# A load of 1 MB moved behind the stores of the query tiles in two cross-attention passes

## The chip, the cores and the metric

The kernel runs on one core of one Trainium2 chip. The metric is the device time of one execution in microseconds, taken as the median of several runs. The core has five engines that work side by side and meet through semaphores: PE (TensorE, the matmuls), DVE (VectorE), ACT (ScalarE), POOL (GpSimd) and SP (SyncE). SP computes nothing: it waits for semaphores and issues DMAs, strictly in the order of its program.

## What is computed

Two sequences of 2048 tokens with 512 channels go through two layers. `x` is (2, 2048, 512) and the context is (2, 77, 512). Cut to what matters, with the conditioning vectors left out:

```
# layer 0: cross-attention
q = ada_ln(x) @ Wq + bq                       # 16 heads of 32
x = x + softmax(q k^T / sqrt(32)) v @ Wp + bp # k, v from the 77 context tokens
# layer 1
q, k, v = split(modulate(ln(x)) @ qkv_w + qkv_b)
x = x + gate * (mha(q, k, v) @ self_o_w + self_o_b)   # 2048 x 2048 self-attention
q = ln(x, g, b) @ q_w + q_b
x = x + mha(q, k_ctx, v_ctx) @ cross_o_w + cross_o_b  # cross-attention again
x = x + gate * (gelu(modulate(ln(x)) @ w1 + b1) @ w2 + b2)
```

## The kernel before

The program is a chain of stages: `conditioning`, `cross_pass` "p1" (layer 0; called pass 1 here), `dense_pass` (q, k and v of the self-attention), `attention`, `cross_pass` "p3" (called pass 3: output projection of the self-attention, then the cross-attention of layer 1) and `mlp`. The change touches `cross_pass` alone, in both of its forms: `own is None` is pass 1, the other form is pass 3.

`cross_pass` works on N = 8 chunks of 512 tokens. A chunk goes through several steps: load of its rows x, (pass 3: projection of the self-attention's output, `own_row`, added to x by `add_own`), statistics and normalisation, turn to channels-first, projection of the queries in four tiles, scores, softmax, weighing of the values, projection of the output, added to x by `add_out`, second normalisation for the next stage. The steps of several chunks are interleaved by hand. Slot m runs the scores of chunk m, the output of chunk m - 1, the projection of the queries of chunk m + 1 and the loads of chunk m + 2. Every engine has its own `slot(m)`, a list of steps in a fixed order, and an engine never goes past a step that waits. The slots of the engines are offset against one another: what DVE does at the start of its slot m + 1 falls into the same time as what SP and PE do at the end of theirs.

x has XR = 3 buffers of 1 MB. Chunks 0 to 2 are loaded ahead of the slots, and `load_x(m + 2)` in the slots m = 1 to 5 loads the chunks 3 to 7: five loads in each pass. `load_x(n)` (L401 to L406) waits until the buffer's former rows are stored and normalised a second time (`xn_done[1]`, a POOL step). Its users are: in pass 1 DVE's `statistics(1, n, 0..3)` (L1138), which stand in DVE's slot n - 1 right behind `query_rest(n-1, 2)`, with `out_rest(n-2, 1)` (L1114) between the first and the second of them; in pass 3 POOL's `add_own_row(n)` (L1418), then DVE's `add_own(n, 0..3)` (L1129).

The queries of a chunk go out and come back through HBM. PE projects a tile (L564), ACT writes its high part into `qo[:, t % 2]` (`query`, L853), DVE the low part (`query_rest`, L1118), and `store_q(n, t)` (L417, 0.5 MB) stores it as soon as `taken["query"]` says so. ACT's `query(n, t)` with t >= 2 waits until the store of tile t - 2 has landed, since they share a buffer. `load_q(n, g)` (L428, three DMAs of 0.25 MB) waits for the landing of the store and loads the tile head by head into `qs[:, g % 2]`, from which PE's `scores` (L590) read. `store_u` (L439 and L440, two DMAs of 0.25 MB) stores the second normalisation's result, after POOL's `rest(2, ...)` (L1428).

On PE, near the end of the slot: `query(m+1,3)`, `turn_weights` of the heads 10 and 11, `turn(2,m-1,1)`, `turn_weights(m,12)` (L601, needs ACT's copy `et` of head 10), `weigh(m,2)` (L610, needs `et` and DVE's `out_rest(m,1)` through the semaphore `os_lo`), `turn_weights(m,13)`, then `scores(m+1,0)`. In pass 3, PE's slot holds `own_row(m+1, 1..3)` (L542 on `p_oi`) between the scores; there are two banks for all projections, and `own_row(n, 2)` needs the bank that DVE's `add_own(n, 0)` frees.

Of the kernel before, what the change touches and what calls it, by code (L numbers as in the profile page):

```python
# [33 lines left out]
def channels(ap):  # L34

    return ap.rearrange("(t p) n -> p t n", p=P)
# [272 lines left out]
def cross_pass(nc, d, name, x_in, x_out, own, k_in, v_in, q_mid, norm_q, norm_u, q_bias, b_out, u_out, raw, preload):  # L309
# [7 lines left out]
    XR = 3  # L317
# [3 lines left out]
    has = lambda n: 0 <= n < N  # L321
# [15 lines left out]
    with nc.cleanup_on_exit(), ExitStack() as ctx:  # L337
# [60 lines left out]
        @block.sync  # L398
        def _(sp):
            def load_x(n):  # L400
                b, i = place(n)  # L401
                if n >= XR:

                    sp.wait_ge(x_stored[n % XR], DMA * (n // XR))
                    sp.wait_ge(xn_done[1], (n - XR + 1) * TT)
                sp.dma_start(x[:, n % XR], x_in[b, i * W:(i + 1) * W, :].rearrange("(t p) c -> p t c", p=P)).then_inc(x_in_s[n % XR], DMA)  # L406

            def load_own(n):
                b, i = place(n)
                if n > 0:  # L410
                    sp.wait_ge(projected["own"], n * TT)
                sp.dma_start(oi.raw[:], o_in[b, :, i * W:(i + 1) * W].rearrange("(t p) w -> p t w", p=P)).then_inc(own_in, DMA)

            def store_q(n, t):
                b, i = place(n)
                sp.wait_ge(taken["query"], n * KT + t + 1)
                sp.dma_start(q_mid[:, b, t * P:(t + 1) * P, i * W:(i + 1) * W].rearrange("s p w -> p s w"),  # L417
                             qo[:, t % 2].bitcast(F32)).then_inc(q_stored[t % 2], DMA)

            def load_q(n, g):  # L420
                b, i = place(n)
                sp.wait_ge(q_stored[g % 2], DMA * ((n * G + g) // 2 + 1))
                if n * G + g >= 2:

                    sp.wait_ge(sm_done, (n * G + g - 1) * TT)
                for row, part in enumerate((0, 0, 1)):
                    src = q_mid[part, b, g * P:(g + 1) * P, i * W:(i + 1) * W].rearrange("(h r) w -> r h w", h=GH)
                    sp.dma_start(qs[row * DH:(row + 1) * DH, g % 2].bitcast(F32), src).then_inc(q_loaded[g % 2], DMA)  # L428

            def store_x(n):  # L430
                b, i = place(n)
                sp.wait_ge(taken["out"], (n + 1) * TT)
                sp.dma_start(x_out[b, i * W:(i + 1) * W, :].rearrange("(t p) c -> p t c", p=P), x[:, n % XR]).then_inc(x_stored[n % XR], DMA)

            def store_u(n, t):
                b, i = place(n)
                r = (n * KT + t) % UR
                sp.wait_ge(u_lo[1], n * KT + t + 1)
                sp.dma_start(u_out[0, b, t * P:(t + 1) * P, i * W:(i + 1) * W], ut.hi[:, r].bitcast(F32)).then_inc(u_stored[r], DMA)  # L439
                sp.dma_start(u_out[1, b, t * P:(t + 1) * P, i * W:(i + 1) * W], ut.lo[:, r].bitcast(F32)).then_inc(u_stored[r], DMA)  # L440

            def slot(m):
                if own is None:
                    if has(m - 3):
                        store_u(m - 3, 3)
                    if has(m):
                        load_q(m, 1)
                        load_q(m, 2)
                    if has(m - 2):
                        store_u(m - 2, 0)  # L450
                    if has(m):
                        store_q(m, 3)
                        load_q(m, 3)
                    if has(m - 2):
                        store_u(m - 2, 1)
                    if has(m - 1):
                        store_x(m - 1)
                    if has(m + 1):
                        store_q(m + 1, 0)
                    if has(m + 2) and m + 2 >= XR:  # L460
                        load_x(m + 2)
                    if has(m - 2):
                        store_u(m - 2, 2)
                    if has(m + 1):
                        store_q(m + 1, 1)
                        load_q(m + 1, 0)
                        store_q(m + 1, 2)
                else:
                    if has(m - 2):
                        store_u(m - 2, 1)  # L470
                    if has(m + 2) and m + 2 >= 1:
                        load_own(m + 2)
                    if m + 2 == CHUNKS:

                        sp.wait_ge(projected["own"], CHUNKS * TT)
                        sp.dma_start(raw.raw[:, 0], channels(own_weight)).then_inc(w_again, DMA)
                    if has(m - 1):
                        store_x(m - 1)
                    if has(m + 1):
                        store_q(m + 1, 0)  # L480
                    if has(m - 2):
                        store_u(m - 2, 2)
                    if has(m + 2) and m + 2 >= XR:
                        load_x(m + 2)
                    if has(m + 1):
                        store_q(m + 1, 1)
                        load_q(m + 1, 0)
                        load_q(m + 1, 1)
                    if has(m - 2):
                        store_u(m - 2, 3)  # L490
                    if has(m + 1):
                        store_q(m + 1, 2)
                    if has(m - 1):
                        store_u(m - 1, 0)
                    if has(m + 1):
                        load_q(m + 1, 2)
                        store_q(m + 1, 3)
                        load_q(m + 1, 3)
                if m == 0:
                    for dst, src in preload:  # L500
                        sp.dma_start(dst, src).then_inc(preloaded, DMA)

            with nc.allow_non_contiguous_dma(reason="short vectors, once"):
                if own is not None:
                    for b in range(B):
                        sp.dma_start(grow[:, b], gate[b].partition_broadcast(P)).then_inc(grow_in, DMA)
                    load_own(0)
                load_x(0)
                for dst, src in small:
                    sp.dma_start(dst, src).then_inc(small_in, DMA)  # L510
                load_x(1)
                for row, part in enumerate((0, 1, 0)):
                    for b in range(B):
                        sp.dma_start(ks[row * DH:(row + 1) * DH, b, :, 0:S].bitcast(F32),
                                     k_in[part, b].rearrange("(h r) s -> r h s", r=DH)).then_inc(ks_in, DMA)
                sp.dma_start(v[0:S], v_in.rearrange("b s c -> s b c")).then_inc(ks_in, DMA)
            load_x(2)
            for m in SLOTS:
                slot(m)
            for r in range(XR):  # L520
                sp.wait_ge(x_stored[r], DMA * len(range(r, N, XR)))
            for r in range(UR):
                sp.wait_ge(u_stored[r], 2 * DMA * len(range(r, N * KT, UR)))
            sp.wait_ge(preloaded, DMA * len(preload))
# [1956 lines left out]
```

## Time and profile before

| | us |
|---|---|
| median of 3 runs | 3903.49 |
| lowest and highest | 3900.64, 3904.45 |
| the profiled execution | 3910.66 |
| its span, from first to last instruction | 3908.9 |
| PE busy in it | 3628.2 (93%) |
| mean granted clock of PE | 0.95 |
| pass 1, about | 87 to 596 |
| pass 3, about | 2600 to 3190 |

A profile tells of one execution; its times are counted from the start of the span. Rows of a timeline give start, duration, engine, line, operation, written tile, read tiles and a count, and in brackets how long the engine had been idle and what ended that. SPq is the queue of SyncE, and its rows are the moments of issue; a merged row (x3) runs from the first issue to the end of the last. In names, `p_` stands for both passes: `p_x` is a chunk's rows, `p_qo` the projected tile, `s_q` its place in HBM, `p_qs` the loaded queries, `p_sm` scores, `p_tr` and `p_et` turned weights, `p_acc` weighed values, `p_os` their two parts, `p_pp` a projection.

### The profile page before, as it was taken

What the parts mean: (1) busy time and instruction counts of PE and PEld (TensorE: products, weight loads), DVE (VectorE), ACT (ScalarE), POOL (GpSimd) and SP (SyncE); (2) the same over time, 40 slices, a digit from 0 to 9 for tenths busy, and PEclk for the clock granted to TensorE, in tenths of its full rate; (3) what the DMA queues carried; (4) which work ended last, traced back from release to release, by engine and by line L of the source; (5) the groups of instructions that cost most, each with busy time, mean ns of one, the idle gap of its engine ahead of it and who ended that gap; (6) DMA issues with size and microseconds to landing.
All of it is one profiled execution on the core that took longest, in us unless ns stands there. A gap on an engine that the chain in (4) does not pass through costs nothing. (4 is left out here: it accounts for less than half of the span.)

```text
span 3908.9 us, 50109 instructions
## 1 busy us (share of the span) xinstructions
PE 3628.2 (93%) x18828; PEld 2403.3 (61%) x18828; DVE 2226.6 (57%) x3964; ACT 1870.3 (48%) x3442; POOL 2132.5 (55%) x1063
## 2 busy tenths in 40 slices
PE   5699988999999999999999999968999969999999
PEld 2577766875555555555555554426777748888887
DVE  2466652266777777777777777614766633222222
ACT  1455552115666666666666666644556532111111
POOL 0456540005898888889888888865677520000000
PEclk8798888999999999999999999987999879999999
DMA  7655657755555555555555554444575661111110
GB/s 231 154 157 149 177 146 221 241 176 141 125 120 120 127 127 132 128 124 118 120 127 130 128 131 103 116 132 110 149 181 157 159 206 58 49 44 44 44 44 33
DMA packets 232009, 505.92 MB, mean 129 GB/s; under 512 B 38199, under 2 KB 55095, under 8 KB 211799
## 3 DMA queue, kind: packets, MB, share of 16 engines
q1 hardware_dynamic: 213335, 368.49, 34.6%
q0 software_dynamic: 18432, 134.23, 15.7%
q8 instruction: 149, 2.44, 0.3%
q14 instruction: 93, 0.76, 0.1%
HBM read 215.54 MB, written 144.51 MB: 92 GB/s over the span
## 5 line engine op out<-in xcount | busy, mean ns | idle before, releaser
L2117 DVE TENSOR_REDUCE first_peak<-first_sm 128x1 f32<-128x512 f32 x1963 | 1211.1, 680 | 358.7 <-PE first_sm L1947 357.5
L2077 ACT ACTIVATE a_e<-a_st 128x512 f32<-128x512 f32 x2048 | 1061.7, 603 | 534.7 <-PE a_st L1966 523.5
L2177 POOL TENSOR_TENSOR a_esum<-a_esum,a_e 128x2048 f32<-128x2048 f32 x256 | 1208.8, 4722 | 18.5
L1966 PE MATMUL a_st<-first_q,first_k 128*128 128x512 f32 x2048 | 825.5, 406 | 16.8 <-ACT a_e L2077 12.0
L1947 PE MATMUL first_sm<-first_k,first_q 96*128 96x512 f32 x1963 | 833.1, 424 | 0.0
L1947 PEld LDWEIGHTS first_sm<-first_k,first_q 96*128 96x128 f32 x1963 | 369.9, 188 | 425.2 <-DVE first_peak L2117 316.2
L1979 PE MATMUL a_acc<-a_e,a_v 128*32 128x512 f32 x4096 | 505.7, 600 | 0.0
L1966 PEld LDWEIGHTS a_st<-first_q,first_k 128*128 128x128 f32 x2048 | 387.6, 190 | 131.2 <-ACT a_e L2077 51.7
L2365 ACT ACTIVATE mlp_gelu<-mlp_ph,mlp_b 128x512 f32<-128x512 f32 x128 | 88.3, 690 | 590.0 <-PE mlp_ph L2327 590.0
L2419 POOL TENSOR_TENSOR mlp_x<-mlp_x,mlp_brow 128x2048 f32<-128x2048 f32 x8 | 39.5, 4934 | 581.7 <-DMA mlp_x<-s_x 581.7
L2327 PE MATMUL mlp_ph<-mlp_us,mlp_w_hi 128*128 128x512 f32 x1024 | 336.6, 391 | 19.2 <-DMA mlp_us<-s_u 19.2
L2380 DVE CAST mlp_gs<-mlp_gelu 128x512 fp32r<-128x512 f32 x128 | 54.8, 428 | 462.2 <-ACT mlp_gelu L2365 462.2
L2339 PE MATMUL mlp_py<-mlp_w_hi,mlp_gs 128*128 128x512 f32 x1024 | 315.3, 389 | 1.8 <-DVE mlp_gs L2382 1.8
L1434 POOL TENSOR_TENSOR p_e<-p_e,p_inv 128x308 f32<-128x308 f32 x256 | 173.4, 711 | 172.0 <-DVE p_inv L1110 172.0
L1979 PEld LDWEIGHTS a_acc<-a_e,a_v 128*32 128x32 f32 x4096 | 100.4, 108 | 220.2 <-ACT a_e L2077 125.1
L2327 PEld LDWEIGHTS mlp_ph<-mlp_us,mlp_w_hi 128*128 128x128 f32 x1024 | 193.5, 189 | 60.0 <-issue 19.6
L590 PE MATMUL p_sm<-p_ks,p_qs 96*128 96x78 f32 x1024 | 170.5, 309 | 53.0 <-DMA p_qs<-s_q 32.2
L2339 PEld LDWEIGHTS mlp_py<-mlp_w_hi,mlp_gs 128*128 128x128 f32 x1024 | 192.1, 188 | 42.0 <-issue 2.1
L590 PEld LDWEIGHTS p_sm<-p_ks,p_qs 96*128 96x128 f32 x1024 | 155.8, 220 | 85.9 <-DMA p_qs<-s_q 31.1
L2327 PE MATMUL mlp_ph<-mlp_us,mlp_raw_lo 128*128 128x512 f32 x512 | 200.2, 391 | 0.0
L2339 PE MATMUL mlp_py<-mlp_raw_lo,mlp_gs 128*128 128x512 f32 x512 | 199.2, 389 | 0.0
L1095 DVE TENSOR_REDUCE p_top<-p_sm 128x4 f32<-128x308 f32 x256 | 118.1, 464 | 138.2 <-PE p_sm L590 136.3
(161 smaller groups left out, 5317.2 us busy)
## 6 DMA issues: line engine op xcount, KB each, us to landing
a_esum_moved<-a_e POOLq DMA_DIRECT2D x128, 1024.0 KB, 7.3
p_qs<-s_q SPq DMA_DIRECT2D x192, 256.0 KB, 5.9
s_q<-p_qo SPq DMA_DIRECT2D x64, 512.0 KB, 7.6
first_k<-s_k SPq DMA_DIRECT2D x24, 1024.0 KB, 11.0
first_q<-s_q SPq DMA_DIRECT2D x96, 256.0 KB, 7.1
s_x<-p_x SPq DMA_DIRECT2D x16, 1024.0 KB, 4.4
s_u<-p_ut_hi SPq DMA_DIRECT2D x64, 256.0 KB, 5.8
s_u<-p_ut_lo SPq DMA_DIRECT2D x64, 256.0 KB, 6.4
```

Source lines behind the costliest of these rows:

```text
L590: mm = pe.matmul(sm[:, unit % 2, h * KE:(h + 1) * KE], qs[0:3 * DH, g % 2, h, qt * P:(qt + 1) * P], ks[0:3 * DH, b, g * GH + h], start=Tru ...
L1095: dve.tensor_reduce(top[:, unit % 4], src, AX.X, ALU.max).then_inc(top_done, 1)
L1434: pool.tensor_tensor(e[:, number % 2, qt, :, 0:S], e[:, number % 2, qt, :, 0:S], inv[:, number % 2, qt].unsqueeze(2).to_broadcast([P, GH, ...
L1947: mm = pe.matmul(sm[:, bank_of_unit(j, u), x * KE:(x + 1) * KE], q[0:3 * DH, j % QR, h, qt * P:(qt + 1) * P], k[0:3 * DH, g % 2, h, kc * K ...
L1966: pe.matmul(st[0:KR, place(kt, h) % RING], k[:, g % 2, h, kt * P:kt * P + KR], q[:, j % QR, h], start=True, stop=True).then_inc(score_done, 1)
L1979: mm = pe.matmul(acc[rows, 0], v[0:KR, g % 2, kt, rows], e[0:KR, (j * NKT + kt) % ER, h], start=(kt == 0), stop=(kt == NKT - 1), tile_posi ...
L2077: act.activation(e[0:KR, (j * NKT + kt) % ER, h], st[0:KR, place(kt, h) % RING], ACT.Exp, scale=SCALE).then_inc(score_read, 1)
L2117: dve.tensor_reduce(dst, src, AX.X, ALU.max).then_inc(unit_read, 1)
L2177: pool.tensor_tensor(esum[:], e[:, slot(0)] if x == 1 else esum[:], e[:, slot(x)], ALU.add).then_inc(e_added, 1)
L2327: mm = pe.matmul(ph[:, m % 4], w1[pw][:, t, m * P:(m + 1) * P], us[:, n % 2, pm, t], start=(t == 0 and s == 0), stop=(t == KT - 1 and s == 2))
L2339: mm = pe.matmul(py[:, tt], gs[:, m % 2, pw, tt * P:(tt + 1) * P], w2[pm][:, m], start=(m == 0 and s == 0), stop=(m == HT - 1 and s == 2))
L2365: act.activation(gelu[:, m % 2], ph[:, m % 4], ACT.Gelu_apprx_tanh, bias=b1[:, m:m + 1]).then_inc(gelu_done, 1)
```

## The change

In both forms of SP's `slot(m)` the call `load_x(m + 2)` moves down. In pass 1 it stood behind `store_q(m+1,0)` and stands behind `store_q(m+1,2)`, as the last of the slot; `store_q(m+1,1)` and `load_q(m+1,0)` also move ahead of `store_u(m-2,2)`. In pass 3 it stood behind `store_u(m-2,2)` and stands behind `store_q(m+1,2)`, ahead of `store_u(m-1,0)`. No instruction is added or taken away, and no wait.

```diff
@@ SP's slot, own is None (pass 1)
                     if has(m + 1):
                         store_q(m + 1, 0)
+                        store_q(m + 1, 1)
+                        load_q(m + 1, 0)
+                    if has(m - 2):
+                        store_u(m - 2, 2)
+                    if has(m + 1):
+                        store_q(m + 1, 2)
                     if has(m + 2) and m + 2 >= XR:
                         load_x(m + 2)
-                    if has(m - 2):
-                        store_u(m - 2, 2)
-                    if has(m + 1):
-                        store_q(m + 1, 1)
-                        load_q(m + 1, 0)
-                        store_q(m + 1, 2)
@@ SP's slot, the other form (pass 3)
                         store_q(m + 1, 0)
                     if has(m - 2):
                         store_u(m - 2, 2)
-                    if has(m + 2) and m + 2 >= XR:
-                        load_x(m + 2)
                     if has(m + 1):
                         store_q(m + 1, 1)
                         load_q(m + 1, 0)
...
                         store_u(m - 2, 3)
                     if has(m + 1):
                         store_q(m + 1, 2)
+                    if has(m + 2) and m + 2 >= XR:
+                        load_x(m + 2)
                     if has(m - 1):
                         store_u(m - 1, 0)
```

## Rows read from the trace of the kernel before

**Rows 1.** The page: the span, and busy time of the engines.

```profile
span 3908.9 us, 50109 instructions
...
PE 3628.2 (93%) x18828; PEld 2403.3 (61%) x18828; DVE 2226.6 (57%) x3964; ACT 1870.3 (48%) x3442; POOL 2132.5 (55%) x1063
```

**Rows 2.** Table of windows: busy us of each engine, granted clock, DMA share.

```profile
core 0: us, PE busy (x) PEld busy (x) DVE busy (x) ACT busy (x) POOL busy (x), PEclk, DMA share, GB/s
212.00:270.00 58.00, 55.68 (x352) 44.44 (x350) 41.98 (x96) 38.36 (x77) 40.02 (x37) 0.97 0.60 164
386.00:444.00 58.00, 53.42 (x289) 42.49 (x288) 35.38 (x78) 33.09 (x65) 33.82 (x33) 0.82 0.63 164
...
2880.00:2940.00 60.00, 56.82 (x328) 45.53 (x326) 37.14 (x78) 34.38 (x65) 41.64 (x40) 0.94 0.69 168
402.50:422.30 19.80, 19.79 (x77) 14.79 (x78) 8.74 (x20) 12.77 (x24) 7.50 (x8) 0.50 0.69 179
2912.00:2920.90 8.90, 8.87 (x42) 8.00 (x43) 6.52 (x12) 3.14 (x7) 2.74 (x3) 0.62 1.05 219
```

**Rows 3.** Table of waits in pass 1: us in total, times, longest.

```profile
ACT p_qo L853 <- DMA s_q<-p_qo: 29.0, 6, 6.4
...
PE p_tr L601 <- ACT p_et L814: 18.4, 8, 4.7
```

**Rows 4.** The same table in pass 3.

```profile
PE p_sm L590 <- DMA p_qs<-s_q: 15.6, 7, 4.2
```

**Rows 5.** Timeline of SyncE's queue, slot 4 of pass 1: start, us.

```profile
389.57 0.37 SPq L406 DMA_DIRECT2D p_x<-in_x  x1
...
391.01 0.87 SPq L417 DMA_DIRECT2D s_q<-p_qo  x1
...
394.26 0.65 SPq L417 DMA_DIRECT2D s_q<-p_qo  x1
...
401.23 1.30 SPq L428 DMA_DIRECT2D p_qs<-s_q  x3
```

**Rows 6.** Timelines of ACT, DVE and PE in the same slot.

```profile
401.29 0.69 ACT L853 ACTIVATE p_qo<-p_pp,p_qb 128x512 fp32r<-128x512 f32 x1 [6.36 <-DMA s_q<-p_qo]
...
389.15 0.74 DVE L1118 SCALAR_TENSOR_TENSOR p_qo<-p_pp,p_qb,p_qo 128x512 fp32r<-128x512 f32 x1
...
395.93 0.69 DVE L1138 BATCH_NORM_STATS2 p_stats<-p_x 128x6 f32<-128x512 f32 x1 [2.08 <-DMA p_x<-in_x]
396.54 0.67 DVE L1114 TENSOR_TENSOR p_os<-p_acc,p_os 128x512 fp32r<-128x512 f32 x1
...
402.51 1.14 PE L601 MATMUL p_tr<-p_ident,p_e 128*77 128x128 f32 x4 [4.58 <-ACT p_et L814]
403.58 1.94 PE L610 MATMUL p_acc<-p_et,p_v 77*32 77x512 f32 x8
```

**Rows 7.** The store of L417 issued at 394.26: its time to landing.

```profile
DMA to landing us min/median/max: 12.2/12.2/12.2
```

**Rows 8.** Timelines of ACT and PE in slot 6, pass 1.

```profile
510.44 0.69 ACT L853 ACTIVATE p_qo<-p_pp,p_qb 128x512 fp32r<-128x512 f32 x1 [1.73 <-PE p_pp L564]
...
512.25 1.06 PE L610 MATMUL p_acc<-p_et,p_v 77*32 77x512 f32 x8
```

**Rows 9.** Timelines, slot 3, pass 3: SyncE, its landing, POOL, DVE, PE.

```profile
2910.99 0.37 SPq L417 DMA_DIRECT2D s_q<-p_qo  x1
...
DMA to landing us min/median/max: 9.9/9.9/9.9
...
2907.31 4.97 POOL L1418 TENSOR_TENSOR p_x<-p_x,p_brow 128x512 f32<-128x512 f32 x4
...
2917.98 0.68 DVE L1129 TENSOR_TENSOR p_x<-p_pp,p_x 128x512 f32<-128x512 f32 x1
...
2912.03 1.08 PE L590 MATMUL p_sm<-p_ks,p_qs 96*128 96x78 f32 x8 [2.37 <-DMA p_qs<-s_q]
...
2922.78 0.48 PE L542 MATMUL p_pp<-p_w,p_oi_hi 128*128 128x512 f32 x1
```

More of the change, by code:

```diff
@@ L482, in slot @@
                         store_u(m - 2, 2)
-                    if has(m + 2) and m + 2 >= XR:
-                        load_x(m + 2)
                     if has(m + 1):
@@ L492, in slot @@
                         store_q(m + 1, 2)
+                    if has(m + 2) and m + 2 >= XR:
+                        load_x(m + 2)
                     if has(m - 1):
```

## Prediction, made before the changed kernel was run

> **What bounds the kernel now.** I read the page first, for where the time lies. TensorE (PE) is busy 93% of a span of 3908.9 us [rows 1], so nearly everything that makes PE wait is paid for. The change touches only `cross_pass`, which runs twice: pass 1 from about 87 to 596 us and pass 3 from about 2600 to 3190 us. The table of windows comes next: in a middle slot PE is busy 53.4 of 58 us in pass 1 and 56.8 of 60 us in pass 3 [rows 2]. Both passes are PE-bound, with little slack for a new stall. The table also gives the granted clock: 0.97 in pass 1's first slot with a load, 0.82 in a later one, 0.94 in pass 3.
>
> The table of waits then says what holds PE: in pass 1 mainly `turn_weights`, behind ACT's copies of `et` (18.4 us in 8 waits), and behind that ACT's `query` step, which waits for a store of `qo` (29.0 us in 6) [rows 3]. In pass 3 PE waits for the load of `qs`, 15.6 us in 7 [rows 4]. So the queue of SyncE (SP) matters, and the timelines of one slot, m = 4 of pass 1, show how. The load of x is issued at 389.57, the store of query tile 1 at 391.01, that of tile 2 at 394.26 [rows 5]. DVE finished tile 1 at 389.15 + 0.74 = 389.89 and gets x at 395.93, 6.3 us after the issue. ACT gets the buffer of tile 1 back only at 401.29, 10.2 us after its store was issued. PE then restarts at 402.51 after 4.58 us idle [rows 6]. Slot m = 6 has no load of x: there ACT waits 1.73 us, for PE, at the same step, and `weigh(m,2)` follows at 512.25 with no gap [rows 8]. So the load ahead of the stores does cost PE time, as the change assumes. What remains is what the load costs when it is late.
>
> **Part by part.** Nothing is added or removed: 5 loads of 1 MB per pass (rows 3 to 7, slots m = 1 to 5) move down SP's list, their two waits with them. Their own waits cost nothing in the new place, since POOL's normalise is done by then.
>
> *Pass 1.* The load moves past `store_q(m+1,1)`, `load_q(m+1,0)` (three DMAs), `store_u(m-2,2)` (two) and `store_q(m+1,2)`: 7 DMAs, 0.5 + 0.75 + 0.5 + 0.5 MB. `store_q(m+1,1)` can go at 389.9, 1.1 us earlier, with no load before it, so its buffer comes back before ACT asks, and the wait of 4.58 us is gone. What is late next is x. The load can be issued only behind `store_q(m+1,2)`, at about 394.7 instead of 389.57 [rows 5]. The transfers in front of it are the ones that were behind it. The queue was busy from 389.57 until tile 2's store landed, 12.2 us after 394.26, at 406.5 [rows 5, 7]. The new order moves the same bytes from 389.9 on, so the last of them, now x, lands at about 406.5 instead of 395.9. DVE's next instruction in order is `statistics(1,m+2,0)`, which needs x, and queued right behind it is `out_rest(m,1)`. Before, that one ended at 396.54 + 0.67 = 397.2, 1.3 us after x landed [rows 6]. PE's `weigh(m,2)` waits for it through `os_lo`, and all the scores of the next slot stand behind `weigh` on PE. So `weigh` goes from 403.58 [rows 6] to 406.5 + 1.3 = 407.8: +4.2 us. The bounds: if x took from its new issue only what it took at the head of the queue, 6.3 us, it would land at 401.0 and `weigh` would come at 402.3, -1.3 us. If the loads of `qs` that now come sooner behind it slow it by another 1 us (my guess), +5.2. I take 4.2, since the queue is full in either order. PE has no slack after that, so 5 x 4.2 = +21 us.
>
> The clock in pass 1: after the stall PE ran 19.8 us at 0.50, its lower level of 1.2 GHz [rows 2]. The later slots pay for such a stretch already, and the new gap of about 9 us keeps it. The first slot ran at 0.97 and would go to about 0.82: 58 x 0.15 = +9 us. Pass 1: +30 us.
>
> *Pass 3.* The load moves past `store_q(m+1,1)`, `load_q(m+1,0)` and `load_q(m+1,1)` (six DMAs), `store_u(m-2,3)` (two) and `store_q(m+1,2)`. In slot m = 3 the stores and loads of q gain, and PE's gap of 2.37 us before `scores` at 2912.03 goes [rows 9]. Tile 2's store landed 9.9 us after 2910.99, at 2920.9. By the same exchange x lands there, less 1 us because the two stores of `store_u(m-1,0)` that shared the queue with it now come later (estimate): 2919.9, where POOL had it in time for 2907.31. POOL is the first user: `add_own_row` takes 4.97 us for its four tiles, so it ends at 2924.9. DVE's `add_own(m+2,0)`, at 2917.98 before, follows and takes 0.68, and PE's `own_row(m+2,2)` needs that to free its bank: 2925.6 against 2922.78 before, +2.9 us [rows 9]. Behind POOL's wait stand `rest(2,m-1,0)` and so SP's `store_u(m-1,0)`, behind that `load_q(m+1,2)`. That load would land some 3 us before its scores, and I cost it at nothing; if that cover goes, each us late is one more on PE. The bounds: if the loads and stores of q go 5 us sooner than now, so that x follows at about 2906 instead of behind 2910.99, and x then takes only the 6.3 us of pass 1 [rows 6], it lands before 2913, `add_own` isn't held and PE keeps its gain. At the other end x lands 1 us later, +3.9. I take +2.9 x 5 = +14.5 us. Against pass 1, this point already contains the gain of the removed gap.
>
> The clock in pass 3: PE finishes what it can (`own_row(m+2,1)`, scores) and then stands some 8 us where it stood 2.4. A restart cost 8.9 x 0.38 = 3.4 us after the short gap in this slot and 19.8 x 0.5 = 9.9 us in pass 1 [rows 2]. I take 4, nearer to pass 3's own row, since dense matmuls follow at once: 5 x 4 = +20 us. Between the ends it is 17 to 50.
>
> The sum: 21 + 9 + 14.5 + 20 = +64 us. The profiled execution took 3910.66 us (span 3908.9 and 1.8 around it), 7.2 above the median 3903.49. The shift is the same for either: 3975 for the profiled one, **3968 us** for the median.
>
> The Trainium skill, "DMA: Bandwidth & Descriptors", section "Rules for kernel authors", says to issue a DMA early and to wait on its semaphore late. That speaks against this change; the trace agrees, since DVE waits about 2 us for x even as issued now [rows 6].
>
> **The rivals.**
> *Faster: the late load still makes it.* Its place is the wait of DVE for x in pass 1 and of POOL in pass 3. It decides at x landing by 403.6 - 1.3 = 402.3 in slot 4, under 7.6 us after its new issue, and by about 2913 in slot 3 of pass 3. For it: at the head of the queue x takes 6.3 us. Against it: nothing of the 2.4 MB in front goes away. At most it gives 4.6 + 58 x 0.18 = 15 us in each of 4 slots, 3 in the first, and about 5 in each of pass 3 (gap and clock): -88, 3815 us. The same page gives, in "Anatomy of one DMA", 2.0 us + bytes / 436 GB/s. By that, as an estimate, the 3.4 MB would be through by 399.7, `weigh` 2.6 us earlier, and with the 25 us of pass 3 the time would be about 3865. The trace disagrees: the same 3.4 MB took 16.9 us from 389.57 to 406.5 [rows 5, 7].
>
> *Only pass 1 pays.* In pass 3 POOL finished 5.7 us before DVE needed it [rows 9]. If x lands by 2913 the 5 x 5 = 25 us of gaps and clock come back there against +30 in pass 1: +5, 3908 us, no change. Against it: the queue is as full as in pass 1.
>
> *Deeper.* Same mechanism, but each restart in pass 3 costs 9.9 us as in pass 1: +64 + 30 = 3998 us. For it: the new idle is longer than any of the present ones in these slots.
>
> That the change doesn't do what it says isn't open: the order of SP's list is the order of issue.
>
> **How the numbers follow.** Forecast 0.72, deeper 0.13, only pass 1 pays 0.06, faster 0.07, and 0.02 that the gains and losses cancel in both. The range holds the forecast's own bounds (pass 1 +2.7 x 5 + 3 and pass 3 +1.4 x 5 + 17, about +41, to about +104): with a little room below, 3930 to 4005 us. A measurement of this kernel can tell about 0.2% (8 us) from no change. Faster 0.07, same 0.08, slower 0.85.
>
> **What would show it.** In pass 1, ACT's wait for `s_q` is nearly gone, DVE's `p_stats` waits for `p_x` some 8 to 12 us in five slots, and PE's gap stands before `weigh` (p_acc, releaser DVE `p_os`) instead of `p_tr`. In pass 3, PE's waits for `p_qs` shrink, POOL idles before L1418 on DMA `p_x`, and DVE before L1129 on POOL. Each load takes 11 to 13 us to land in place of 6 to 7. The prediction is wrong if the load still lands in about 7 us, if `out_rest(m,1)` ends by 402, or if PE's clock is no lower in pass 3.

## The result and the profile after

The changed kernel takes 3963.2 us (median of 4 runs, 3957.37 to 3968.75) against 3903.4 us (4 runs, 3900.64 to 3904.45): a ratio of 1.0151, with a 95% interval of 1.0134 to 1.0169. It is 59.8 us slower. Its profiled execution took 3957.37 us, the lowest of its runs, and the profile of before took 3910.66, above its median. So the two profiles differ by 46.7 us of span, less than the medians do. Every window below is from one execution of its kernel: where two kernels run the same code, the windows of five slots differ by 1 to 3 us (pass 1 of the kernel with only pass 3 changed took 275.20 us, where before took 277.39).

The page of after: span, busy time of the engines.

```profile
span 3955.6 us, 50109 instructions
...
PE 3626.5 (92%) x18828; PEld 2403.4 (61%) x18828; DVE 2227.0 (56%) x3964; ACT 1869.4 (47%) x3442; POOL 2132.2 (54%) x1063
```

Every engine works as long as before [rows 1] and PE within 2 us: the time is waiting. To see where, I cut both passes from the store of tile 0 in slot m = 1 to the same store in slot m = 6, the five slots with a load. First before, then after; the first row of each is pass 1, the second pass 3. The columns are those of rows 2.

```profile
222.47:499.86 277.39, 257.89 (x1442) 205.52 (x1441) 177.76 (x386) 165.93 (x320) 170.03 (x161) 0.86 0.62 167
2771.84:3082.83 310.99, 291.64 (x1682) 234.46 (x1681) 201.86 (x408) 181.89 (x339) 221.92 (x201) 0.96 0.65 166
```

```profile
222.05:529.54 307.49, 258.65 (x1442) 206.88 (x1441) 177.89 (x386) 165.71 (x320) 169.83 (x161) 0.82 0.57 151
2796.95:3132.61 335.66, 291.44 (x1682) 232.88 (x1681) 201.21 (x408) 181.71 (x339) 221.87 (x201) 0.92 0.63 154
```

The counts of matmuls are equal (1442 and 1682), so each pair is the same work. Pass 1 grew by 30.1 us: PE's idle time went from 19.5 to 48.8, its busy time by 0.8. Pass 3 grew by 24.7: idle from 19.4 to 44.2, busy -0.2. The mean granted clock is lower, 0.82 for 0.86 and 0.92 for 0.96, and yet the same matmuls took no longer: this mean counts the idle time too.

The table of waits shows who waits now. Pass 1 of after, then pass 3 (us in total, times, longest):

```profile
DVE p_stats L1138 <- DMA p_x<-in_x: 63.2, 5, 13.4
PE p_acc L610 <- DVE p_os L1114: 47.0, 5, 10.2
...
ACT p_qo L853 <- DMA s_q<-p_qo: 2.4, 1, 2.4
```

```profile
POOL p_x L1418 <- DMA p_x<-s_x: 54.8, 5, 13.0
DVE p_x L1129 <- POOL p_x L1418: 52.9, 6, 11.1
PE p_pp L542 <- DVE p_x L1129: 35.9, 6, 8.9
```

ACT's wait for the stores of `qo` fell from 29.0 us [rows 3] to 2.4, which is what the change buys. The price stands in the other rows. Slot m = 4 of pass 1 in after, SyncE, the landing of the load of x issued at 414.20, then DVE and PE:

```profile
405.94 4.19 SPq L417 DMA_DIRECT2D s_q<-p_qo  x2
410.23 1.78 SPq L428 DMA_DIRECT2D p_qs<-s_q  x3
...
413.73 0.37 SPq L417 DMA_DIRECT2D s_q<-p_qo  x1
414.20 0.51 SPq L406 DMA_DIRECT2D p_x<-in_x  x1
...
DMA to landing us min/median/max: 12.7/12.7/12.7
...
426.90 0.69 DVE L1138 BATCH_NORM_STATS2 p_stats<-p_x 128x6 f32<-128x512 f32 x1 [13.20 <-DMA p_x<-in_x]
427.51 0.67 DVE L1114 TENSOR_TENSOR p_os<-p_acc,p_os 128x512 fp32r<-128x512 f32 x1
...
428.33 1.94 PE L610 MATMUL p_acc<-p_et,p_v 77*32 77x512 f32 x8 [9.93 <-DVE p_os L1114]
```

The chain is read from the bottom: PE's `weigh` waits for DVE's `out_rest`, and that stands in DVE's order behind `statistics`, which waits 13.20 us for x. Before, x came 6.3 us after its issue and DVE waited 2.08 us [rows 5, 6]. Slot m = 3 of pass 3, POOL, DVE and PE:

```profile
2958.33 4.92 POOL L1418 TENSOR_TENSOR p_x<-p_x,p_brow 128x512 f32<-128x512 f32 x4 [12.98 <-DMA p_x<-s_x]
2963.28 0.69 DVE L1129 TENSOR_TENSOR p_x<-p_pp,p_x 128x512 f32<-128x512 f32 x1 [11.12 <-POOL p_x L1418]
2964.02 0.80 PE L542 MATMUL p_pp<-p_w,p_oi_hi 128*128 128x512 f32 x1 [8.87 <-DVE p_x L1129]
```

In place of the gap of 2.37 us before the scores [rows 9] PE has one of 8.87 us before `own_row`. PE's waits for `qs` in this pass fell from 15.6 us in 7 [rows 4] to 4.5 in 4.

### The profile page after: what moved, and what is told of

Its sections match the earlier page's. It is cut to its first block and busy times, and to the rows that moved or that the text cites. A ratio compares the mean times of both kernels' runs of the same rounds, so it can differ in the third digit from the quotient of the medians.

```text
span 3955.6 us, 50109 instructions
## 1 busy us (share of the span) xinstructions
PE 3626.5 (92%) x18828; PEld 2403.4 (61%) x18828; DVE 2227.0 (56%) x3964; ACT 1869.4 (47%) x3442; POOL 2132.2 (54%) x1063
## 5 line engine op out<-in xcount | busy, mean ns | idle before, releaser
L2327 PEld LDWEIGHTS mlp_ph<-mlp_us,mlp_w_hi 128*128 128x128 f32 x1024 | 193.4, 189 | 59.6 <-issue 19.4
L814 ACT ACTIVATE p_et<-p_tr 77x512 f32<-77x512 f32 x256 | 148.1, 588 | 123.1 <-PE p_tr L601 67.1
```

Source lines behind the costliest of these rows:

```text
L814: act.activation(et[0:S, number % HR], tr[0:S, number % 2], ACT.Copy).then_inc(et_done, 1)
L2327: mm = pe.matmul(ph[:, m % 4], w1[pw][:, t, m * P:(m + 1) * P], us[:, n % 2, pm, t], start=(t == 0 and s == 0), stop=(t == KT - 1 and s == 2))
```

## Experiments

Each ratio is against runs of the kernel before on the same chip, whose medians were 3903.3 to 3907.0 us. All edits are against the kernel before, unless it says otherwise.

**One pass at a time.** Theory: the losses of the passes are separate and add up, about 28 us in pass 1 and 20 in pass 3. Rival: only pass 1 pays, or most lies in pass 3. Pass 1 alone:

```diff
                         store_q(m + 1, 0)
-                    if has(m + 2) and m + 2 >= XR:
-                        load_x(m + 2)
+                        store_q(m + 1, 1)
+                        load_q(m + 1, 0)
                     if has(m - 2):
                         store_u(m - 2, 2)
                     if has(m + 1):
-                        store_q(m + 1, 1)
-                        load_q(m + 1, 0)
                         store_q(m + 1, 2)
+                    if has(m + 2) and m + 2 >= XR:
+                        load_x(m + 2)
                 else:
```

> The kernel before, with the load moved in pass 1 alone. My theory: the late load holds DVE's statistics, out_rest behind them and PE's weigh, 4.9 us a slot in the changed kernel's trace, and the passes don't touch each other. The queries of pass 1's first slot and of pass 3's first slot stand 28 us further apart in the changed kernel's trace, so +28 us, about 3931 us (3925 to 3937). PE's wait for p_os shows 47 us in 5 waits, and pass 3 keeps its five waits for p_qs. Rival: the two passes share a cause (the state in which pass 1 leaves the chip, or the clock), and one alone gives clearly more or less than its part; then this one lies outside 3920 to 3942.

Measured: 3934.86 us, ratio 1.0083 (1.007 to 1.0097), +30.8.

Pass 3 alone:

```diff
                         store_u(m - 2, 2)
-                    if has(m + 2) and m + 2 >= XR:
-                        load_x(m + 2)
                     if has(m + 1):
...
                         store_q(m + 1, 2)
+                    if has(m + 2) and m + 2 >= XR:
+                        load_x(m + 2)
                     if has(m - 1):
```

> The kernel before, with the load moved in pass 3 alone. My theory: the load holds POOL's add_own_row, DVE's add_own and PE's own_row(.,2). The prediction gave this pass +34 us (14.5 of shift and 20 of clock); the changed kernel's trace shows only 19 to 22 us between the start of pass 3 and the start of the mlp, since each restart ran on the low clock for 3 to 5 us and not for 8. So +20 us, 3923 us. Rival: the profiled execution understates it (the median of the changed kernel moved by 60 us, its profile by 47), and this run shows +30 or more. Sum of this run's shift and pass 1's: between 47 and 60 us.

Measured: 3928.44 us, ratio 1.0071 (1.0059 to 1.0084), +24.4. The waits of the two kernels, pass 1 alone and then pass 3 alone, over the whole span:

```profile
DVE p_stats L1138 <- DMA p_x<-in_x: 61.9, 5, 14.1
PE p_acc L610 <- DVE p_os L1114: 46.7, 6, 10.9
```

```profile
POOL p_x L1418 <- DMA p_x<-s_x: 54.3, 5, 12.8
PE p_pp L542 <- DVE p_x L1129: 37.0, 6, 8.7
ACT p_qo L853 <- DMA s_q<-p_qo: 28.0, 6, 6.6
```

Each kernel has the waits of its own pass and not those of the other, and 30.8 + 24.4 = 55.2 us is near the 59.8 of the change. The passes are separate and both pay, pass 3 somewhat more than the 20 us expected. In pass 1 the change also lets `store_q(m+1,1)` and `load_q(m+1,0)` go ahead of `store_u(m-2,2)`. No run separates that from the load's move; it is the wait for x that the rows show. The same five slots of pass 3 took 335.51 us in the kernel with pass 3 alone and 312.05 in the one with pass 1 alone, +23.5, as the pair above.

**Is it the order on DVE?** If the stall reaches PE only because `out_rest` is queued behind `statistics`, exchanging the two removes it. Against the changed kernel, in DVE's part of pass 1:

```diff
-                    if has(m + 1):
-                        statistics(1, m + 1, 0)
                     if has(m - 1):
                         out_rest(m - 1, 1)
                     if has(m + 1):
+                        statistics(1, m + 1, 0)
                         statistics(1, m + 1, 1)
```

> The changed kernel, with one step of DVE moved in pass 1: out_rest(m-1,1) ahead of the first statistics(1,m+1,0), which waits for x. My theory: weigh isn't held by x any more, PE's wait for p_os (47 us in 5) goes, and the stall moves on to the next step behind the statistics, the first unit_max of the next slot: PE waits before the third scores for ACT's p_e instead. DVE gets to that unit_max at x + 3.2 us, where in the changed kernel PE had only reached its scores at x + 5; so 2 to 3.5 us less per slot, -10 to -17 us against the changed kernel: 3946 to 3953 us. Rival: PE's stall isn't due to this chain but to something else that is late at the same time (the queries' load, the clock): then the gap stays before weigh and the time at 3963 us.

Measured: 3949.5 us, ratio 1.0119 (1.0106 to 1.0133), 13.7 below the changed kernel. Slot m = 4, PE, then the five slots of pass 1:

```profile
409.52 1.06 PE L610 MATMUL p_acc<-p_et,p_v 77*32 77x512 f32 x8
...
422.27 1.08 PE L590 MATMUL p_sm<-p_ks,p_qs 96*128 96x78 f32 x4 [8.92 <-ACT p_e L806]
...
222.91:513.95 291.04, 247.99 (x1442) 197.74 (x1441) 177.41 (x386) 166.59 (x320) 170.09 (x161) 0.86 0.59 159
```

`weigh` has no gap any more, so the link `statistics` to `out_rest` to `weigh` is the one that held it. But DVE still stands for x (59.4 us in 5, against 63.2), now one instruction later. `unit_max` and `unit_sub` of the next scores are behind it, ACT's `p_e` behind those, and PE waits 8.92 us there. DVE, which keeps its order, passes its wait on through whatever is queued behind: only the first link changed. PE's idle time in the five slots fell by only 5.7 us (48.8 to 43.1). The larger part of the gain is busy time, 258.65 to 247.99 us for the same 1442 matmuls, because less of the work runs at the lower clock: about 76 us of PE's busy time in the changed kernel's five slots, about 55 here. I had expected the gain from the shorter stall alone, so its size is in part luck.

**Place or bytes?** Two kernels cut the ten later loads of x to one of their four row tiles (0.25 MB of 1 MB). The other three tiles of those rows stay as an earlier slot left them. The cut, made in the changed kernel and in the kernel before:

```diff
-                sp.dma_start(x[:, n % XR], x_in[b, i * W:(i + 1) * W, :] ...
+                tiles = 1 if n >= XR else TT
+                sp.dma_start(x[:, n % XR, 0:tiles], x_in[b, i * W:i * W + tiles * P, :] ...
```

> The changed kernel, but each of the ten later loads of x brings only one of its four row tiles, 0.25 MB; three quarters of the rows of the chunks 3 to 7 are left as the buffer had them, so that part of the result is left out. Everything that waits, waits for the same semaphores at the same places. My theory: x is late by what is in front of it and by its own share of the queue. In the changed kernel it landed 4.1 us behind tile 2's store in slot 4 of pass 1, and about 3 us behind it in pass 3; a quarter of the bytes takes 3.1 and 2.3 us off that. 5 x 3.1 + 5 x 2.3 = -27 us: 3936 us (3928 to 3945), still some 30 above the kernel before, which is the place itself. Rival: the flight is a fixed latency and the bytes in front of the load, its own size doesn't count: 3960 us. Second rival: bytes are all that counts, and with a quarter the kernel is back near 3904 us.

> The kernel before, with the same cut of the later loads to 0.25 MB (three quarters of the later rows left out of the computation), the load in its first place. This is the price of the load ahead of the stores, which the change set out to save. My theory: tile 1's store lands 3.1 us sooner, ACT's wait of 6 us for s_q falls to 3, and PE's gaps of 4.65, 3.70, 4.58 and 3.27 us in pass 1 to about 1; the clock stays as it is, since the run with the load behind tile 1 had gaps of 1 us and the same low stretches. In pass 3 the waits for p_qs (2.1 us on average) go. 4 x 3 + 5 x 2 = -22 us: 3882 us (3870 to 3892). Rival: the clock comes back too where the gap is gone, 10 us in each slot: 3850 us.

Measured: the late small load takes 3922.11 us, ratio 1.005 (1.0036 to 1.0064), 41 below the changed kernel and 19 above the kernel before. The early small load takes 3858.86 us, ratio 0.9886 (0.987 to 0.9902), 44 below the kernel before. Both are misses by size: I expected 3936 us (3928 to 3945) and 3882 us (3870 to 3892), and the bytes were worth more. The waits with the late small load:

```profile
DVE p_stats L1139 <- DMA p_x<-in_x: 43.3, 5, 9.8
POOL p_x L1419 <- DMA p_x<-s_x: 37.3, 5, 8.6
PE p_acc L611 <- DVE p_os L1115: 27.9, 6, 6.5
PE p_pp L543 <- DVE p_x L1130: 19.3, 6, 4.6
```

With a quarter of the bytes DVE's wait per slot fell only from 12.6 to 8.7 us (63.2 / 5 and 43.3 / 5). The loads themselves say the same. In pass 1 the early load lands in 6.3 us in the median when full and in 3.0 when small, the late one in 12.1 and in 8.1. What remains is the queue in front: the place alone costs the kernel at both sizes, 59.8 us with the full load and 63.3 with the small one (3922.11 - 3858.86). So three quarters of the bytes of x are worth 41 to 44 us in either place, and its place 60 to 63 us. That the two worths of the bytes are so near is no rule. In the ten slots (both passes) the late load's 41.7 us are 37.1 of PE's idle time and 4.6 of busy time. The early one's 46.7 are 19.0 of idle and 27.7 of busy: there the clock came back, as the rival of that run had it (3850 us).

**Only past tile 1.** If the gain of the change is that tile 1's store no longer stands behind the load, the load should move past that store and little else: in pass 1 past that store alone, in pass 3 past the load of query group 0 too.

```diff
                         store_q(m + 1, 0)
+                        store_q(m + 1, 1)
                     if has(m + 2) and m + 2 >= XR:
                         load_x(m + 2)
+                    if has(m + 1):
+                        load_q(m + 1, 0)
                     if has(m - 2):
                         store_u(m - 2, 2)
                     if has(m + 1):
-                        store_q(m + 1, 1)
-                        load_q(m + 1, 0)
                         store_q(m + 1, 2)
...
-                    if has(m + 2) and m + 2 >= XR:
-                        load_x(m + 2)
                     if has(m + 1):
                         store_q(m + 1, 1)
                         load_q(m + 1, 0)
+                    if has(m + 2) and m + 2 >= XR:
+                        load_x(m + 2)
+                    if has(m + 1):
                         load_q(m + 1, 1)
```

> Both passes: the load stands behind the store of tile 1 only (and in pass 3 behind the load of query group 0 too), ahead of everything else of the slot. My theory: it is the place in the queue that counts on both sides. Tile 1's store lands before ACT asks for its buffer, so PE's wait of 3 to 5 us in turn_weights goes in four slots of pass 1, with the low clock behind it (0.18 of 58 us each), and x lands 2 to 3 us after it did at first, near 398 in slot 4, before weigh is due. In pass 3 the waits for p_qs go. About -45 us, 3858 us (3830 to 3880); the prediction put the most that can be had at -88. Rival: any delay of x behind its first place costs (DVE already waits 2 us for it); then weigh comes later than before and the kernel is slower than 3903 us.

Measured: 3894.38 us, ratio 0.9973 (0.9962 to 0.9983). It is faster, but by only 9.7 us where I expected 45: a miss. DVE and PE in slot m = 4, then the five slots of pass 1:

```profile
395.93 0.69 DVE L1140 BATCH_NORM_STATS2 p_stats<-p_x 128x6 f32<-128x512 f32 x1 [4.23 <-DMA p_x<-in_x]
...
397.36 1.06 PE L612 MATMUL p_acc<-p_et,p_v 77*32 77x512 f32 x8 [0.96 <-DVE p_os L1116]
...
221.21:491.19 269.98, 259.13 (x1442) 207.84 (x1441) 177.98 (x386) 165.98 (x320) 170.13 (x161) 0.85 0.66 172
```

The gap of 4.58 us shrank to 0.96, and PE's idle time in the five slots from 19.5 to 10.9. But the clock stays at 0.85 and the busy time at 259, so in this pass what should have come back with the gap, the clock, didn't. Pass 3 gave as much: its five slots took 303.31 us for 310.99, PE busy 286.37 for 291.64, at a clock of 0.98 for 0.96. Two versions follow. One puts `out_rest(m-1,1)` ahead of `statistics` besides, by the edit shown above:

> The load behind tile 1's store as in the run before, and in pass 1 also DVE's out_rest(m-1,1) ahead of the first statistics. That run had PE idle 1.65, 1.07, 1.33, 0.96 and 2.72 us before weigh, for p_os. My theory: these 7.7 us go, but the next thing late is the load of query group 0 (a gap of 1.2 us for p_qs already stood in one slot), which gives half of it back; the low clock behind stays. -4 us against the run with the load behind tile 1: 3890 us (3880 to 3896). Rival: the low stretches of 14 to 17 us are due to the gap before weigh and go with it, 7 us a slot: 3860 us.

Measured: 3891.9 us, ratio 0.9968 (0.9955 to 0.9981), inside the expected range: 11.4 us below before, for 9.7 with the load's place alone, which these intervals don't tell apart. In the trace the gaps before `weigh` are gone and others have come, in nine places, for the queries. PE's waits in pass 1, and the five slots:

```profile
PE p_sm L592 <- DMA p_qs<-s_q: 14.4, 9, 2.6
...
221.77:487.57 265.80, 252.24 (x1442) 201.43 (x1441) 178.31 (x386) 165.61 (x320) 169.93 (x161) 0.88 0.66 175
```

The other moves the load past `load_q(m+1,0)` too in pass 1, and all of `statistics` behind `unit_sub(m,1)` on DVE:

```diff
                         store_q(m + 1, 0)
+                        store_q(m + 1, 1)
+                        load_q(m + 1, 0)
                     if has(m + 2) and m + 2 >= XR:
                         load_x(m + 2)
...
                         query_rest(m, 2)
-                    if has(m + 1):
-                        statistics(1, m + 1, 0)
                     if has(m - 1):
                         out_rest(m - 1, 1)
...
                         unit_sub(m, 1)
+                    if has(m + 1):
+                        statistics(1, m + 1, 0)
...
+                        spread(1, m + 1)
                     if has(m - 1):
                         out_rest(m - 1, 2)
```

> In pass 1 the load stands behind tile 1's store and the three loads of query group 0, and DVE's statistics of the new rows stand behind the next slot's first two unit_sub, with out_rest ahead of them; pass 3 as in the run with the load behind tile 1. My theory: neither tile 1's buffer, nor the queries, nor x is awaited any more at the end of a slot in pass 1, so it looks as slot 6 of the kernel before, without a gap and with a low stretch of 3.4 us: 7.7 us of gaps and 4 x 5 to 7 us of clock less than with the load behind tile 1, 3862 us (3850 to 3880). Rival: the statistics now hold up ACT's inverse_root and with it exponential(m,2): the stall only moves, and the time is that of the run with the load behind tile 1 or above, 3890 to 3905 us.

Measured: 3893.06 us, ratio 0.9967 (0.9956 to 0.9979), a miss. I had put `statistics` ahead of `out_rest(m-1,2)`, and `weigh` was held again one group later, in all five slots. DVE, then PE:

```profile
399.63 2.46 DVE L1139 BATCH_NORM_STATS2 p_stats<-p_x 128x6 f32<-128x512 f32 x4
402.13 0.38 DVE L1148 BATCH_NORM_AGGREGATE p_mv<-p_stats 128x2 f32<-128x6 f32 x4
402.43 0.66 DVE L1115 TENSOR_TENSOR p_os<-p_acc,p_os 128x512 fp32r<-128x512 f32 x1
...
403.24 1.94 PE L611 MATMUL p_acc<-p_et,p_v 77*32 77x512 f32 x8 [2.89 <-DVE p_os L1115]
```

This time it isn't x: DVE waits for it only once in the five slots, 0.6 us. What holds `out_rest` is the work in front of it, 2.46 us for the four tiles of `statistics` and 0.38 for `spread`.

**Both orders together.** Here `statistics` stands behind both `out_rest` and `query_rest(m,3)` on DVE. In pass 1 SP issues `store_q(m+1,0)`, `store_u(m-2,2)`, `store_q(m+1,1)`, `load_q(m+1,0)`, the load of x, `store_q(m+1,2)`; pass 3 has the load behind `load_q(m+1,0)` as above.

```diff
                         query_rest(m, 2)
-                    if has(m + 1):
-                        statistics(1, m + 1, 0)
                     if has(m - 1):
                         out_rest(m - 1, 1)
-                    if has(m + 1):
-                        statistics(1, m + 1, 1)
...
                         query_rest(m, 3)
+                    if has(m + 1):
+                        statistics(1, m + 1, 0)
...
+                        spread(1, m + 1)
+                    if has(m):
                         unit_max(m, 2)
```

> As the run before it with the load behind query group 0, with its mistake mended: there the statistics also stood ahead of out_rest(m-1,2), and PE waited 2.9 us before weigh in each of five slots for that. Here they stand behind out_rest(m-1,2) and query_rest(m,3), and in pass 1 the two stores of store_u(m-2,2) go out between the stores of tile 0 and tile 1, where the queue is nearly empty. My theory: no step of PE waits for x in pass 1, the gaps of 2.9 us go, and with them the low stretches of 7 to 14 us shrink to some 3 to 7, as they did with the small load. 5 x 2.9 + 5 x 3 = -30 us against that run: 3864 us (3852 to 3880). Rival: the loads of query group 1 and the statistics, now later, are awaited instead, and the time stays at 3885 to 3895 us.

The same edit of DVE's order alone, in the kernel before:

> The kernel before with only DVE's order of the last run (statistics behind out_rest(m-1,2) and query_rest(m,3) in pass 1), SP's queue untouched. My theory: there PE waits for ACT's buffer of tile 1, not for DVE, so it is 3903 us within 8 us, and a gain of the last run comes from the two edits together. Rival: the order of DVE is worth the gain by itself; then this run is below 3885 us.

Measured: both together 3887.41 us, ratio 0.9958 (0.9945 to 0.9971), the lowest median of the kernels that compute everything, though its interval overlaps those of the three before it. DVE's order alone 3911.95 us, ratio 1.0018 (1.0008 to 1.0028): no gain, rather a small loss. So DVE's order alone doesn't give the 19.6 us. How much the load's place gives without it isn't shown: this place of the load with DVE's old order was not run, and the run with -9.7 us had another place. The five slots of pass 1 with both, and the slot that now waits:

```profile
226.32:483.67 257.35, 236.14 (x1442) 189.91 (x1441) 176.98 (x386) 165.82 (x320) 170.02 (x161) 0.93 0.68 180
...
404.29 1.07 PE L592 MATMUL p_sm<-p_ks,p_qs 96*128 96x78 f32 x4 [3.83 <-DMA p_qs<-s_q]
```

PE idles 21.2 us here, more than before the change, but its matmuls take 236.1 us instead of 257.9, at a clock of 0.93. What waits now is the load of query group 1, 3.8 to 5.0 us in four slots: it stands behind the load of x. I expected 3864 us and got what the rival said. In these kernels PE always waits for something in pass 1: with the load behind tile 1's store for x (7.7 us in five waits), with the DVE step moved for `qs` (14.4 us in nine), and here for `qs` (17.3 us in four).

## Why the prediction came out right, and where its steps didn't

The forecast was 3968 us, and 3963.2 was measured. By its steps:

**Where x lands: held.** The prediction let x take the last place of a full queue: 11 to 13 us after its issue. Before, the ten loads took 6.0 to 7.4 us. In after the ten loads took 11.5, 12.9, 11.3, 12.7 and 12.1 us in pass 1 and 10.8, 11.6, 13.9, 11.4 and 13.4 in pass 3. That the same 3.4 MB pass in nearly the same time in either order is what carried the result: in slot m = 4 of pass 1 it was 16.9 us before, and 17.1 in after (tile 1's store is issued at 409.78, x lands 12.7 us after 414.20). DVE's wait, 12.6 us on average, was a little longer than the 8 to 12 foretold.

The rival by a page's rate, 3865 us, let x land at 399.7, 5.0 us after its issue at 394.7. It is out: the shortest of the ten took 10.8. The Trainium skill gives that rate in "DMA: Bandwidth & Descriptors", section "Anatomy of one DMA", for one DMA of GpSimd's software path. These loads go through SyncE's queue, with others in front, so the runs refute the use of the rate here and not the page. The advice of the Trainium skill (same page, "Rules for kernel authors") to issue early and wait late agrees with the trace of the change: a load issued later cost 59.8 us. It isn't the whole of it: with the load only behind tile 1's store it is issued later too, and the kernel is 9.7 us faster.

**Pass 1, forecast +30: measured +30.1 in the five slots, +30.8 by the run of that pass alone.** PE's `weigh(m,2)` began at 236.33, 288.98, 345.24, 403.58 and 460.03 before, and at these times after:

```profile
243.25 1.08 PE L610 MATMUL p_acc<-p_et,p_v 77*32 77x512 f32 x4 [8.75 <-DVE p_os L1114]
305.60 1.08 PE L610 MATMUL p_acc<-p_et,p_v 77*32 77x512 f32 x4 [10.19 <-DVE p_os L1114]
366.43 1.08 PE L610 MATMUL p_acc<-p_et,p_v 77*32 77x512 f32 x4 [8.70 <-DVE p_os L1114]
```

The last two are 428.33 and 489.90. The lag grows by 6.9, 9.7, 4.6, 3.6 and 5.1 us from slot to slot. The forecast was 4.2 in each, with 9 more in the second step for the clock of the first slot. So the size was right where PE was already held before (4.4 on average in the last three), and the first two steps were near. The stretch between the first two of these starts, before and then after:

```profile
236.33:288.98 52.65, 47.11 (x289) 37.54 (x288) 35.47 (x77) 33.53 (x66) 33.97 (x32) 0.94 0.67 174
```

```profile
243.25:305.60 62.35, 51.26 (x288) 41.09 (x289) 35.57 (x78) 33.01 (x64) 34.00 (x32) 0.83 0.57 150
```

The clock fell as forecast (0.83 for 0.82), but PE's busy time rose by 4.2 us, not 9; the other 5.5 are idle time. Over all five slots the busy time rose by only 0.8, since the later ones got some back. The term was priced as 58 us of work at a lower mean clock, but part of the low clock falls into the idle time, where it costs nothing.

**Pass 3, forecast +34.5: measured +24.7 in the slots, 24.4 by the run of that pass alone.** The chain is the one foretold: POOL waits for x, DVE for POOL, PE for DVE, and `add_own_row` took 4.92 us for 4.97. In slot m = 3 `own_row(m+2,2)` came 30.82 us after its slot's store of tile 0, against 27.57 before: +3.25, forecast 2.9. The first mis-sized term is the clock, 4 us for each restart, 20 in all. PE's busy time for the same 1682 matmuls didn't change (291.6 and 291.4). After the gap in slot m = 3 of after the clock was back within 3.5 us:

```profile
2964.00:2967.50 3.50, 3.48 (x8) 2.80 (x9) 3.46 (x6) 0.00 (x0) 2.81 (x4) 0.51 0.71 148
2967.50:3000.00 32.50, 31.57 (x190) 25.38 (x190) 24.04 (x57) 21.44 (x41) 23.16 (x23) 1.00 0.59 146
```

That is 3.5 x 0.49 = 1.7 us, in place of 3.4 that the same slot had already lost at 2912 before [rows 2]. The forecast added a gross price where the kernel before was paying it too. The sign that it named, a lower clock in pass 3, came (0.92 for 0.96) and cost nothing, so it was no test of this term. The second is the idle term, which was too small: +24.9 us over five slots against 14.5. From store to store of tile 0 the five slots grew by 4.3, 8.6, 5.2, 0.3 and 6.3 us; I had worked from the third alone. The two errors are of opposite sign, 20 too much and 10 too little, so part of the closeness of the total is luck. The lower end of the range has a flaw too: it is added up from +2.7 us a slot in pass 1 and +1.4 in pass 3, which are worked out nowhere and lie above the lower bounds given with the steps (-1.3, and a slot of pass 3 that keeps its gain). The measurement lies well inside either way.

**What the sum of the profiles leaves.** 30.1 + 24.7 = 54.8 us in the slots, 46.7 in the spans. Most of the rest lies in pass 3 outside the five slots. From its first `own_row` to the store of slot 1, where both kernels run the same code, before took 150.25 us and after 146.08. From slot 6 to the first matmul of the `mlp` it was 116.37 and 113.38:

```profile
3082.83:3199.20 116.37, 76.51 (x391) 55.90 (x389) 45.33 (x89) 48.93 (x86) 40.67 (x38) 0.74 0.58 154
```

```profile
3132.61:3245.99 113.38, 75.44 (x390) 55.09 (x389) 45.39 (x89) 48.87 (x86) 40.71 (x38) 0.75 0.59 158
```

24.7 - 4.2 - 3.0 = 17.5 us for the pass. Of the 3.0, 1.7 is a wait for `qs` that fell from 4.22 to 2.51. The 4.2 can't be put down to the change. PE idles as long in both (21.3 and 21.6 us), and its busy time differs, 128.97 and 124.52, at a clock of 0.83 and 0.86. In the twelve profiles of this document that stretch, with the same code in it, takes from 146.1 to 152.9 us, and 151.3 in one of the kernels with the late load. That the medians differ by 59.8 is in keeping with it, and not resolved further.

**The rivals.** *Faster* fell with x landing at 426.9, not before `weigh`. *Only pass 1 pays* fell with the second run. *Deeper* fell with PE's busy time in pass 3, which didn't grow. That the wait of ACT went and did give PE something isn't refuted: moving the load past tile 1's store (in pass 3 past the load of query group 0 too), and no further, gained 9.7 us. What the change got wrong is how far.

## What to carry to other kernels

When a transfer is moved down a full queue, work out its landing from the sum in front and its own size, not from its own size alone: here 12.1 us for 1 MB behind the rest, 8.1 for a quarter of it, against 6.3 and 3.0 at the head. Then follow its first consumer's in-order queue, since each instruction behind the wait carries it on to its own readers, and moving one of them out of the way gained only 13.7 of 59.8 us, since the next was of the same kind. Compare stretches of equal instruction counts, idle and busy apart: a lower mean clock cost nothing where it fell into the idle time (0.86 to 0.82, busy time +0.8 us), and a price per restart must be set against the one already paid.

## What was not expected of the hardware

The granted clock in pass 1 hardly follows the size of the gap. With gaps of about 1 to 2.7 us and the load past tile 1 the five slots ran at 0.85, as before with one gap of 1.4 us and four of 3.3 to 4.7 (0.86). With the early small load, idle time was the same 11 us (252.12 - 240.94) and the clock 0.93:

```profile
222.86:474.98 252.12, 240.94 (x1442) 193.41 (x1441) 177.26 (x386) 165.49 (x320) 170.01 (x161) 0.93 0.63 168
```

And with both orders it was 0.93 too, at 21 us of idle time. 17 to 23 us of PE's time in pass 1 hang on this (258 or 259 against 241 or 236 us for the same 1442 matmuls), and no run here shows what decides it. The place of the gap has a part in it. Two pairs of kernels differ in the same exchange on DVE alone, which moves gaps from before `weigh(m,2)` to before the scores: the changed kernel and the one with `out_rest` first (PE busy 258.65 and 247.99 us), and the two with the load past tile 1 (259.13 and 252.24). The five slots have the same 1442 matmuls in all four, and the idle time hardly differs within a pair (48.8 and 43.1, 10.9 and 13.6). Why the place matters is open. Nor does the length of a gap tell how long the lower level, 1.2 GHz, lasts behind it. In slot m = 4 of after PE restarted at 428.33, after 9.93 us, and ran at it for 16.7 us; after 8.87 us in pass 3 it was 3.5:

```profile
428.30:445.00 16.70, 16.67 (x68) 12.49 (x69) 10.80 (x27) 10.89 (x21) 4.19 (x5) 0.50 0.25 57
```
